# Fused convolution and attention kernel: V's tap weights copied from GpSimd, queries made without copies, thin stages set between dense ones

## What is computed

```python
# layer 0: multi-scale linear attention
qkv = conv1x1(x, w_qkv)                                    # 384 channels
agg = conv1x1(depthwise5x5(qkv, w_dw), w_pw, groups=48)    # 48 groups of 8 channels
qkv = concat([qkv, agg]).reshape(B, 32 heads, 24, 256)
q, k, v = relu(qkv[:, :, :8]), relu(qkv[:, :, 8:16]), qkv[:, :, 16:]
v = pad(v, one row of ones)
vk = einsum('bhdn,bhen->bhde', v, k)
out = einsum('bhde,bhen->bhdn', vk, q)
x1 = x + conv1x1(out[:, :, :-1] / (out[:, :, -1:] + 1e-15), w_proj)
# layer 1: full attention over 256 pixels, D = 64
theta, phi = W_theta x1 + b_theta, W_phi x1 + b_phi
f = softmax(theta^T phi / 8)
out = x1 + W_fuse (f x1) + b_fuse
```

## Time and profile before

| | |
|---|---|
| median of 3 runs | 67.39 us (66.37 to 68.16) |
| the profiled execution | 66.49 us, of which its span is 64.7 us |
| PE busy | 56.2 us, 87% of the span, 998 matmuls |
| PE weight loads | 41.5 us, 998 |
| DVE busy | 40.3 us, 62% |
| ACT busy | 24.5 us, 38% |
| POOL busy | 14.8 us, 23% |
| TensorE clock granted | full over the whole span |

### The profile page before, as it was taken

One profiled execution on the slowest core, in us unless ns is written; L12 is line 12 of the kernel. 1 busy time (PEld: TensorE's weight loads), 2 busy tenths in 40 slices (PEclk: granted clock), 3 DMA queues, 4 the chain that ended last, 5 costly groups with the idle time before them and its releaser, 6 DMA issues.

```text
span 64.7 us, 2307 instructions
## 1 busy us (share of the span) xinstructions
PE 56.2 (87%) x998; PEld 41.5 (64%) x998; DVE 40.3 (62%) x101; ACT 24.5 (38%) x53; POOL 14.8 (23%) x22
## 2 busy tenths in 40 slices
PE   2999999999999899997828299599999999889940
PEld 2759987699765567564504056478998579666830
DVE  3638599989984922026104969055886369896460
ACT  0923949009693806021000000624010509996300
POOL 4401000399999997000000000000000000000000
PEclk9999999999999999999999999999999999999999
DMA  0695261389428999242999000000000000000242
GB/s 0 191 225 154 52 170 43 90 180 283 95 71 221 239 260 237 73 143 57 220 154 110 6 10 0 0 0 10 0 0 0 0 5 0 0 0 0 89 162 83
DMA packets 6074, 5.88 MB, mean 91 GB/s; under 512 B 2080, under 2 KB 5680, under 8 KB 6064
## 3 DMA queue, kind: packets, MB, share of 16 engines
q1 hardware_dynamic: 5008, 4.46, 29.2%
q10 hardware_dynamic: 1024, 1.25, 7.6%
q0 software_dynamic: 32, 0.02, 0.2%
HBM read 1.19 MB, written 0.52 MB: 27 GB/s over the span
## 4 chain that ended last, share of the span: by engine, by line
PE 41%; SPq 19%; DVE 13%; ACT 10%; DMA 9%; issue 4%; DVEq 0%; ACTq 0%
DMA rq<-conv 9%; SPq L382 8%; PE bank L984 6%; ACT pr L551 6%; SPq L404 6%; PE bank L761 5%; SPq L400 4%; PE bank L805 3%; DVE toks L581 3%; PE bank L862 3%; PE bank L784 3%; PE bank L817 3%; PE bank L1007 3%; PE bank L1048 3%; PE bank L872 2%
## 5 line engine op out<-in xcount | busy, mean ns | idle before, releaser
L817 PE MATMUL bank<-planes,wpair 64*32 64x256 f32 x288 | 9.6, 391 | 0.0
L805 PE MATMUL bank<-planes,wlast 32*32 32x256 f32 x288 | 6.9, 397 | 0.8 <-issue 0.7
L817 PEld LDWEIGHTS bank<-planes,wpair 64*32 64x32 f32 x288 | 5.2, 105 | 3.4 <-issue 1.3
L784 PE MATMUL bank<-wqkv_t,xp 128*128 128x128 f32 x48 | 6.4, 283 | 0.0
L784 PEld LDWEIGHTS bank<-wqkv_t,xp 128*128 128x128 f32 x48 | 5.8, 194 | 0.7 <-issue 0.4
L470 ACT ACTIVATE toks<-bank 128x512 f32<-128x512 f32 x4 | 4.1, 1140 | 4.1 <-PE bank L784 4.1
L805 PEld LDWEIGHTS bank<-planes,wlast 32*32 32x32 f32 x288 | 3.9, 103 | 2.7 <-issue 1.6
L527 ACT ACTIVATE m<-bank 128x512 f32<-128x512 f32 x1 | 0.6, 597 | 11.6 <-PE bank L862 11.6
L761 PE MATMUL bank<-warm 128*128 128x256 f32 (+1 forms) x8 | 3.5, 587 | 1.2 <-DVE warm L566 1.2
L479 ACT ACTIVATE planes<-bank 128x512 f32<-128x512 f32 x6 | 3.8, 651 | 1.7 <-DVE planes L590 0.9
L551 ACT ACTIVATE pr<-bank,nmx 128x256 f32<-128x256 f32 x8 | 3.7, 476 | 1.8 <-DVE nmx L723 1.7
(11 more groups left out here) (112 smaller groups left out, 103.3 us busy)
## 6 DMA issues: line engine op xcount, KB each, us to landing
planes<-planes SPq DMA_DIRECT2D x10, 180.0 KB, 3.3
xs<-in_x ACTq DMA_DIRECT2D x2, 256.0 KB, 3.3
rq<-q_relu SPq DMA_DIRECT2D x4, 128.0 KB
wpair<-wnext SPq DMA_DIRECT2D x10, 48.0 KB, 2.8
out<-ys SPq DMA_DIRECT2D x3, 128.0 KB, 2.0
planes<-planes ACTq DMA_DIRECT2D x2, 180.0 KB, 3.4
rq<-conv ACTq DMA_DIRECT2D x2, 128.0 KB, 4.4
rq<-conv SPq DMA_DIRECT2D x2, 128.0 KB, 5.4
```

What stands on the lines that cost most here:

```text
L784: last = nc.tensor.matmul(bank[:, TOK[kind][pair], a * P:(a + 1) * P], xp[:, pair, a, :], wqkv_t[:, kind, :], start=True, stop=True)
L805: last = nc.tensor.matmul(bank[32 * quad:32 * (quad + 1), i, 0:NPIX], wlast[rows, kind, quad, u, :], window(rows, which, quad, u, 2), star ...
L817: last = nc.tensor.matmul(bank[32 * quad:32 * (quad + 1), 2 * h + j, 0:NPIX], wpair[rows, kind, j, quad, u, :], window(rows, plane_set(kin ...
```

## The change

Five things change.

- **Plain queries by products.** Instead of `by_pixel(Q, pair)` (four products of 128x128, tokens on the partitions), PE makes one product of 128x512 per pair with the weights standing still, which gives Q with channels on the partitions (`plain_queries`). ACT (pair 0) and DVE (pair 1) copy it to a new tile `qp`.
- **Query tokens by transposes.** `query_tokens` makes the Q tokens with eight transposes of `qp`, between `by_pixel(V, 0)` and `by_pixel(V, 1)`. ACT now copies V's first tokens ahead of Q's.
- **No plain query copies.** ACT rectifies `qp` straight into `rq[:, 0]` in two instructions, after the copy of the convolved K. The rectifying copies from PSUM on ACT and DVE, the tile `q_relu` and SP's four transfers are gone.
- **V's pair copies on GpSimd.** The four transfers of V's first-column weights go from SP to GpSimd, right after their weights are made and ahead of the `kt0` and `vt0` work.
- **Order on PE and DVE.** `by_token(K)` and `denominators(0)` go behind the pairs of Q, `value_keys(0)` behind the first round of V's pairs, `projected_sums(0)` between the second and third rounds. DVE runs `guard(0)` and `reciprocals(0)` ahead of the masks of `value_keys(0)`. The denominators' bank is 5 instead of 6. The diff, cut, goes through SP, POOL, ACT, DVE and PE in this order:

```diff
-        q_relu = sb("q_relu", P, SEGS, PIX)
+        qp = sb("qp", P, 2, PHASES, P)
...
-        WL = 4
+        WL, Q0 = 4, (4, 5)
...
-        DEN = 6
+        DEN = 5
...
-            for kind in (Q, V):
-                sp.wait_ge(plane_act[kind], 2)
-                twins(kind, 0)
-                sp.wait_ge(plane_dve[kind], 2)
-                twins(kind, 1)
-            sp.wait_ge(wconv_pool[V], 3)
-            for i in range(QUADS):
-                sp.dma_start(*pair_copy(V, i)).then_inc(pair_moved[V], 16)
-            sp.wait_ge(q_relu_act, 1)
-            sp.wait_ge(q_relu_dve, 1)
-            for quad in range(QUADS):
-                sp.dma_start(*plain_queries(quad)).then_inc(rq0_moved, 16)
+            sp.wait_ge(plane_act[Q], 2)
+            twins(Q, 0)
+            sp.wait_ge(plane_dve[Q], 2)
+            twins(Q, 1)
+            sp.wait_ge(plane_act[V], 2)
+            twins(V, 0)
+            sp.wait_ge(plane_dve[V], 2)
+            twins(V, 1)
             sp.wait_ge(conv_act, 2)
...
             nc.gpsimd.tensor_tensor(*column_weights(V, 2, wlast[:, V]), ALU.mult).then_inc(wconv_pool[V], 1)
+            pool.wait_ge(wconv_pool[V], 3)
+            for i in range(QUADS):
+                pool.dma_start(*pair_copy(V, i)).then_inc(pair_moved[V], 16)
...
             second_plane(1)
+            act.wait_ge(q0_mm, 1)
+            nc.scalar.activation(qp[:, 0].rearrange("p f n -> p (f n)"), bank[:, Q0[0], :], ACT.Copy).then_inc(qp_act, 1)
...
+            tokens(V, 0)
             tokens(Q, 0)
-            tokens(V, 0)
             plane(Q, 0)
             plane(Q, 1)
-            act.wait_ge(plane_dve[Q], 2)
-            nc.scalar.activation(*relu_bank(0), ACT.Relu).then_inc(q_relu_act, 1)
             plane(V, 0)
             plane(V, 1)
             conv_first_rounds(K, 1)
+            for pair in range(2):
+                act.wait_ge((qp_act, qp_dve)[pair], 1)
+                nc.scalar.activation(rq[:, 0, :, pair * P:(pair + 1) * P], qp[:, pair], ACT.Relu).then_inc(rq0_out, 1)
             act.wait_ge(wl_mm, 1)
...
             relu_keys(1)
+            dve.wait_ge(q0_mm, 2)
+            nc.vector.tensor_copy(qp[:, 1].rearrange("p f n -> p (f n)"), bank[:, Q0[1], :]).then_inc(qp_dve, 1)
             tokens(Q, 1)
...
-            dve.wait_ge(plane_act[Q], 2)
-            nc.vector.tensor_scalar_max(*relu_bank(1), 0.0).then_inc(q_relu_dve, 1)
             plane(V)
...
+            guard(0)
+            reciprocals(0)
             for n in range(2):
                 for c in range(2):
                     attend_sums(0, n, c)
-            guard(0)
-            reciprocals(0)
...
+            def plain_queries(pair):
+                src = xp[:, pair].rearrange("c f n -> c (f n)")
+                nc.tensor.matmul(bank[:, Q0[pair], :], wqkv_t[:, Q, :], src, start=True, stop=True).then_inc(q0_mm, 1)
+
+            def query_tokens(pair):
+
+                pe.wait_ge((qp_act, qp_dve)[pair], 1)
+                for a in range(PHASES):
+                    last = nc.tensor.transpose(bank[:, TOK[Q][pair], a * P:(a + 1) * P], qp[:, pair, a, :], ident[:, :])
+                last.then_inc(tok_mm[Q], 1)
...
             pe.wait_ge(wt_out, 2)
-            by_pixel(Q, 1)
+            plain_queries(1)
             pe.wait_ge(plane_act[K], 4)
             pe.wait_ge(k_relu_out, 2)
             by_pixel(V, 0)
+            query_tokens(0)
+            query_tokens(1)
             by_pixel(V, 1)
...
             convolve_pairs(Q, range(0, 3))
 
+            pe.wait_ge(plane_act[V], 2)
+            pe.wait_ge(plane_dve[V], 2)
+            by_token(K, 0, TR_K, tr_k_mm)
+            by_token(K, 1, TR_K, tr_k_mm)
+            pe.wait_ge(rq0_out, 2)
+            pe.wait_ge(ks_out, 2)
+            denominators(0)
+            pe.wait_ge(wconv_pool[V], 4)
+            pe.wait_ge(conv_act, 2)
+            pe.wait_ge(conv_dve, 2)
+            convolve_last_column(V)
+            pe.wait_ge(pair_moved[V], 16 * QUADS)
+            pe.wait_ge(twin_moved[V], 16 * QUADS)
+            convolve_pairs(V, range(0, 1))
             pe.wait_ge(wproj_out, 1)
...
-            convolve_pairs(V, range(1, 3))
+            convolve_pairs(V, range(1, 2))
             pe.wait_ge(vk_zero, 4)
             pe.wait_ge(vk_out[0], 4)
             projected_sums(0, 0)
             projected_sums(0, 1)
+            convolve_pairs(V, range(2, 3))
```

25 lines of the change are left out of this document (2 added, 23 removed).

## The result

The changed kernel takes 69.38 us in the median of 4 runs (68.80 to 70.81), the kernel before 66.93 us in the same session (66.37 to 68.16). The ratio is 1.037 (95%: 1.031 to 1.042): **slower**, by 2.5 us, where 66.7 us and a range up to 68.1 were forecast. Single runs of one kernel lie some per cent above its others (the kernel before from 66.17 to 71.26 us over 21 runs); ratios here are without those. The profiled execution took 68.92 us with a span of 67.1 us, against 66.49 and 64.7 us.

The account below looks back on a forecast made before the run. PE was taken as bound by dense work, waits and pauses for instruction blocks. Pairs of Q end 1.3 us late, the middle gains; spread moves from 41.49 to 40.85, -0.65 us, giving 66.7 us from median 67.39, range 65.1 to 68.1.

Parts of the forecast that it names:

- Front: Up to the pairs of Q: query tokens copied 1.99 us later; pairs of K at 19.95, pairs of Q at 26.24.
- The twins: Transfers ahead of the pairs of Q: fourth lands at 25.8 after 3.3 us, hidden by 0.4 us.
- First boundary: Load 74 of the pairs of Q: PE out of instructions, pause 0.7 us until the next block; end 29.9.
- New wait: Before V's last column: PE waits 0.7 us for ACT's copy of the convolved Q, behind the kt1 copies.
- Second boundary: Load 88 of V's last column: crossed at 34.2, next instruction block due at 33.2, so no pause.
- there 4.0 us after the last boundary: PE's instruction fetch: estimate that the next block arrives 4.0 us after the last boundary when transfers are as busy.
- Gathers: Ahead of denominators(1): issued from 32.2, landing in 3.9 us at 36.75, wait 0.25 us.
- rival of slow gathers: Gathers take 5.70 us, landing at 38.55, 1.8 late; spread at 42.2, total 68.1 us; chance 0.15.
- Second round, end: V's second round of pairs to spread: round 1.0 us plus pause 0.45, ending 38.75; spread at 40.85.
- The 0.69 us before `spread`: Wait ahead of spread behind ACT's copy of projected_sums(0): claimed gone, the copy lying under V's third round.
- copies on GpSimd: V's pair copies moved to POOL: costed at nothing, weights landing at 27.2 while V's pairs start at 34.4.
- no-pause rival: PE's instruction blocks come in under 3 us, so pauses go: spread at 39.45, -2.05 us, 65.3 us; chance 0.33.

Follow-up runs that it names:

- e12_swap_fill6_keys: Changed kernel plus six tiny matmuls before Q's last column, ACT's convolved-Q copy ahead of kt1 copies, DVE's key sum behind plane copies; 66.18 us, 0.978.
- e13_wait_first: Changed kernel with two PE wait lines exchanged, so the late semaphore for ACT's convolved-Q copy is named first; 67.51 us, 0.999.
- e4_pool_only: Kernel before with V's pair copies on GpSimd and nothing else; 65.94 us, 0.972.
- e7_query_no_order: Changed kernel with PE's and DVE's order of the kernel before; 67.72 us, 0.998.
- e3: Changed kernel with the four gathers held back until V's last column has ended; 73.86 us in one run.
- e1: Changed kernel with ACT's copy of the convolved Q and its gathers ahead of the kt1 copies; 67.49 us in the profiled execution.
- e8: Kernel before with V's pair copies on GpSimd and the third round of V's pairs behind the plain heads' projected sums; 65.89 us, 0.964.
- e14: Changed kernel with the late semaphore named first, ACT's convolved-Q copy ahead of kt1 copies, and DVE's late key sum; 67.65 us median (65.25 to 68.98).
- e9_fill1: Changed kernel with one tiny matmul ahead of the last column of Q; 70.46 us in one run.
- e10_fill3: Changed kernel with three tiny matmuls ahead of the last column of Q; 70.1 us in one run.
- e15_pool_order_held: Kernel before with V's copies on GpSimd, new order, and denominators(0)'s late plain-query wait named second instead of first; 69.08 us in one run.

## Why the prediction was wrong

The changed kernel's times against its steps:

- **Front: right.** Pairs of K at 19.77 (19.95 forecast), last column of Q at 23.68 (23.88), pairs of Q at 26.39 (26.24). The twins weren't hidden by 0.4 us, PE waited 0.27 for them: they landed in 4.0 us in the median, where 3.3 had been taken. `e12_swap_fill6_keys` confirms that DVE's chain carries it.
- **First boundary: right.** At load 74 as computed, pause 3.50 - 2.93 = 0.57 us (0.7), pairs of Q over at 29.8 (29.9).
- **New wait: right.** 0.70 us (0.7), V's last column from 32.19 (32.25).
- **Second boundary: the step that failed.** "Its boundary (load 88 of 96) is crossed at 34.2, and the block for it was due at 33.2: no pause". The boundary was at load 89 and was reached at 33.8, but the block was there at 36.55. The rule "there 4.0 us after the last boundary" came from two intervals between boundaries, with no wait inside them, and was then used over a wait. Packet, its duration and the 1.43 us behind it are 1.15 + 1.38 + 1.43 = 4.0 us in the kernel before, and 4.74 + 1.59 + 1.43 = 7.8 us here. The term was 0 and measured 4.95 - 2.13 = 2.8 us, the whole difference to the forecast of `spread` (2.78 us). The wait of 0.7 us was priced, but not that the packet of the next block would start only behind it. `e13_wait_first` shows what the late semaphore's place in the separate instruction was worth: 1.9 us of idle time and 69.38 to 67.51 us. But there too the block came 5.8 us after the last boundary (34.88 - 29.06), not 4.0. It cost little only because PE spent 0.66 us of that time in the wait itself. So of the 3.8 us by which the rule failed about 2 go with that place, and about 1.8 have no shown cause.
- **Gathers: SP's right, ACT's too dear.** SP's landed in 3.9 to 4.0 us (3.9 forecast), ACT's in 3.0 to 3.2, and with PE late there was no wait instead of 0.25 us. The rival of slow gathers (5.7 us) didn't come about.
- **Second round, end: right.** Its pause is 0.50 us, as 39.88 to 41.46 is 1.58 us (0.45 forecast), with the block 3.9 us after the last boundary: over dense work the rule held once more. The 0.69 us before `spread` are gone.
- **What the parts are worth: attributed wrongly.** The prediction costed the copies on GpSimd at nothing and saw the gain in the removed plain query copies. `e4_pool_only` and `e7_query_no_order` show -2.8% for the former and about +2.7% for the latter: SP's queue was the resource that mattered.
- **The no-pause rival** (65.3 us, 0.33) had the sign of the pauses wrong. Three boundaries of the changed kernel cost 0.57, 2.8 and 0.50 us, while the two ahead of these, which by the count lie 126 and 252 loads before the first of them (in the last column of Q and the pairs of K), left no gap in the weight loads. A pause longer than 1.17 us stood in the text as a reason for "slower", with too little weight: 0.12 together with the gathers.

## What to carry to other kernels

In a kernel whose engine runs many short instructions, mark where it stops with nothing as releaser, and when a wait is moved behind such a place, look for the next stop too: here a wait of 0.70 us came with a pause of 2.23 us behind it. If several semaphores guard one instruction, try naming the one that comes last first, so that it rides on the instruction; in `e13_wait_first` that changed no work and was worth 3.7%. Time the smallest part of a change alone before the large one: four transfers moved to another queue gave 2.8% by themselves, and the rearranged queries that were to bring the gain cost 1.8 us.

## What the hardware did that I had not expected

- With a separate semaphore instruction of 1.45 us ahead of V's last column, the packet on q8 started 1.03 us after its end with the rings idle (e3) and 1.39 us after it with the gathers in them (changed). With the same wait on the weight load (0.66 us in e13) it started inside the wait, at 32.04.
- From the end of the packet to PE going on passed 1.43 (before), 1.43 (changed), 1.36 (e3), 1.48 (e1) and 1.52 us (e13), with busy and with idle rings; it was longer in e4 (1.57), e8 (1.75) and e14 (1.77).
- GpSimd issued the four pair copies in 0.50 us each, where 0.75 had been taken, and they landed in 1.8 to 3.2 us.
- A long pause was followed by a lower clock in some runs. After PE's 2.23 us idle in `e9_fill1` the granted clock of the stretch 39 to 41 us was 0.50, and `value_keys(0)` took 1.98 us, against 1.16 in the changed kernel:

```profile
39.00:41.00 2.00, 2.00 (x72) 1.80 (x64) 0.00 (x0) 0.00 (x0) 0.00 (x0) 0.50 0.03 0
```

  In `e10_fill3`, after 2.26 us idle, it was 0.50 from 37 to 39 us. The changed kernel, with the same pause of 2.23 us, was granted 1.00 in every stretch from 33 to 43 us, so the pause alone doesn't explain it. In `e15_pool_order_held`, after 3.15 us idle, the stretches from 32.7 to 38 us were at 0.50.
